# A two-layer transformer kernel: the second half's input normalisations on another engine, four low parts on VectorE, and a new table of places

## What is computed

```python
x = L0_attn_x                                  # (4, 256, 512) float32
xn = layernorm(x)
h = xn @ Win.T + bin                           # the small model: width 64, 4 layers
for l in range(4):
    h = h + sconv(silu(layernorm(h)), l) * sc_lin[l]      # a decaying complex scan
    h = h + silu(layernorm(h) @ W1[l].T + b1[l]) @ W2[l].T + b2[l]
small = layernorm(h) @ Wout.T + bout
hidden = silu(xn @ gate.T * gate_s) * (xn @ up.T * up_s)   # 1792 wide, codes -1, 0, 1
x = x + small + (hidden @ down.T) * down_s
xn = layernorm(x)
z = (silu(xn @ U1 @ V1g + b1g) * (xn @ U1 @ V1u + b1u)) @ U2 @ V2 + b2
x = x + xn @ (weight * block_mask).T + bias + z
```

## Time and profile before

| what | value |
|---|---|
| median of three runs | 305.38 us |
| profiled execution, its own time | 305.49 us |
| its span, first to last instruction | 303.6 us |
| TensorE busy | 291.7 us, 96% |
| VectorE busy | 175.8 us, 58% |
| GpSimd busy | 159.2 us, 52% |
| ScalarE busy | 118.4 us, 39% |
| mean granted TensorE clock | 0.977 of full |

### The profile page before, as it was taken

One profiled execution on the slowest core, in us unless ns is written; L12 is line 12 of the kernel. 1 busy time (PEld: TensorE's weight loads), 2 busy tenths in 40 slices (PEclk: granted clock), 3 DMA queues, 4 the chain that ended last, 5 costly groups with the idle time before them and its releaser, 6 DMA issues.

```text
span 303.6 us, 4378 instructions
## 1 busy us (share of the span) xinstructions
PE 291.7 (96%) x1573; PEld 194.3 (64%) x1573; DVE 175.8 (58%) x270; ACT 118.4 (39%) x197; POOL 159.2 (52%) x184
## 2 busy tenths in 40 slices
PE   6888989999999999999999999989999999999995
PEld 4785547665565657556565655646577888788784
DVE  3784796565725784684545745678887622333303
ACT  1552345453634132444635535223045730146500
POOL 4878259995391311155474284630467585047650
PEclk9795899999999999999999999999999999999999
DMA  7999618108000212010110011210020000200003
GB/s 256 328 286 208 101 35 124 33 1 121 2 0 2 69 36 71 0 35 13 37 35 26 2 35 38 69 35 2 0 69 1 3 1 32 73 35 0 0 2 138
DMA packets 11749, 17.86 MB, mean 59 GB/s; under 512 B 848, under 2 KB 6224, under 8 KB 11728
## 3 DMA queue, kind: packets, MB, share of 16 engines
q1 hardware_dynamic: 6624, 12.49, 12.7%
q0 software_dynamic: 4960, 4.98, 10.1%
q10 hardware_dynamic: 144, 0.12, 0.1%
HBM read 20.46 MB, written 2.10 MB: 74 GB/s over the span
## 4 chain that ended last, share of the span: by engine, by line
PE 85%; POOL 6%; DVE 4%; issue 2%; DMA 1%; ACT 1%; DVEq 0%; POOLq 0%
PE bank L593 15%; PE bank L594 15%; PE bank L690 15%; PE bank L561 8%; PE bank L563 8%; PE bank L562 8%; PE bank L652 5%; PE bank L624 3%; PE bank L630 2%; PE bank L555 2%; DMA early<-in_params 1%; PE bank L643 1%; PE bank L642 1%; PE bank L615 1%; POOL root L1079 1%
## 5 line engine op out<-in xcount | busy, mean ns | idle before, releaser
L1162 POOL TENSOR_TENSOR hidl<-hid,hidh 128x512 f16<-128x512 f32 x28 | 33.3, 1189 | 47.8 <-ACT hidh L756 47.6
L593 PE MATMUL bank<-xh,gatew 128*128 128x512 f16 (+1 forms) x136 | 45.5, 353 | 2.6 <-ACT XT L785 1.4
L594 PE MATMUL bank<-xl,gatew 128*128 128x512 f16 (+1 forms) x136 | 45.4, 353 | 0.0
L593 PE MATMUL bank<-xh,upw 128*128 128x512 f16 (+1 forms) x136 | 44.8, 348 | 0.0
L594 PE MATMUL bank<-xl,upw 128*128 128x512 f16 (+1 forms) x136 | 44.8, 348 | 0.0
L690 PE MATMUL bank<-downw,hidh 128*128 128x512 f16 x112 | 42.5, 380 | 0.0
L690 PE MATMUL bank<-downw,hidl 128*128 128x512 f16 x112 | 42.4, 379 | 0.0
L1168 POOL TENSOR_TENSOR actl<-hid,acth 128x512 fp32r<-128x512 f32 (+1 forms) x22 | 28.7, 1307 | 25.9 <-ACT acth L763 25.7
L1079 POOL TENSOR_TENSOR root<-var,powers 128x4 f32<-128x4 f32 (+1 forms) x25 | 23.6, 949 | 23.5 <-DVE var L942 19.9
L830 ACT ACTIVATE silu<-bank,early 128x512 f32<-128x512 f32 x28 | 19.2, 687 | 41.1 <-PE bank L594 41.1
L1011 DVE SCALAR_TENSOR_TENSOR hid<-bank,early,silu 128x512 f32<-128x512 f32 x28 | 21.0, 751 | 19.8 <-PE bank L594 19.3
(11 more groups left out here) (158 smaller groups left out, 607.1 us busy)
## 6 DMA issues: line engine op xcount, KB each, us to landing
X<-in_x SPq DMA_DIRECT2D x8, 256.0 KB, 5.6
out_x<-X SPq DMA_DIRECT2D x8, 256.0 KB, 2.0
downw<-in_down POOLq DMA_DIRECT2D x2, 896.0 KB, 8.3
stage<-in_v SPq DMA_DIRECT2D x6, 256.0 KB, 2.6
stage<-in_mask SPq DMA_DIRECT2D x4, 256.0 KB, 7.0
upw<-in_up POOLq DMA_DIRECT2D x1, 1024.0 KB, 11.9
gatew<-in_gate POOLq DMA_DIRECT2D x1, 1024.0 KB, 12.5
stage<-in_weight SPq DMA_DIRECT2D x4, 256.0 KB, 2.6
```

Source lines behind the costliest of these rows:

```text
L593: pe.matmul(bank_of(key)[:, c], w, xh[b][:, k, c], start=(k == 0), stop=False)
L594: mm = pe.matmul(bank_of(key)[:, c], w, xl[b][:, k, c], start=False, stop=(k == KT - 1))
L1162: pool.tensor_tensor(hidl[:, n % FT, :], hid[:, n % UNITS, :], hidh[:, n % FT, :], ALU.subtract).then_inc(hid_lo, 1)
```

## The change

- The four normalisations of block 1 in layer 0 move from VectorE to ScalarE, as an Identity activation with a scale (the root) and a bias (minus mean times root). VectorE makes minus the mean, GpSimd multiplies by the root (tile nmr).
- The low parts of units 0 to 3 move from GpSimd to VectorE, each behind the hid of the next unit, with a semaphore of their own (first_lo).
- The constants ahead of the first transpose are 15 instead of 11, and three more (FILL) stand ahead of the first pass.
- PROLOGUE is written anew; `rows` and `centre win` are in it now. All tables of places have new numbers.
- SyncE waits for the first casting load of gate codes before it issues the fifth staged load and what is behind it.

```diff
-    place(W2_AT, [[("rows",), ("centre", "win")], [("centre", "w2")]])
+    place(W2_AT, [[("centre", "w2")]])
...
-PROLOGUE = ((("seed", 0), ("stats", 0), ("stats", 1), ("norm", 0), ("seed", 1), ("norm", 1), ("stats", 2)),
-            (("xt", 0), ("codes", 0), ("load", 0), ("norm", 2), ("seed", 2), ("stats", 3), ("grow", 0)),
+PROLOGUE = ((("stats", 0), ("stats", 1), ("load", 0), ("norm", 0), ("seed", 0), ("stats", 2), ("norm", 1), ("seed", 1)),
+            (("xt", 0), ("codes", 0), ("norm", 2), ("seed", 2), ("stats", 3), ("grow", 0)),
             (("xt", 1), ("codes", 1), ("first", 0, 0), ("norm", 3), ("load", 1), ("grow", 1)),
-            (("xt", 2), ("first", 0, 1), ("xcopy", 0), ("first", 1, 0), ("grow", 2), ("grow", 3)),
-            (("xt", 3), ("first", 1, 1), ("xcopy", 1), ("first", 2, 0), ("first", 2, 1), ("xcopy", 2),
+            (("xt", 2), ("rows", 0), ("first", 0, 1), ("xcopy", 0), ("first", 1, 0), ("grow", 2), ("grow", 3)),
+            (("xt", 3), ("centre", 0), ("first", 1, 1), ("xcopy", 1), ("first", 2, 0), ("first", 2, 1), ("xcopy", 2),
              ("first", 3, 0), ("first", 3, 1), ("xcopy", 3)))
-WARM = 11
+WARM = 15
+FILL = 3
...
-LOAD_AT = (0.2, 0, 7.1, 16.2)
-GROW_AT = (0, 0, 0.1, 0.5, 0.5, 0.5)
-LN_AT = (0.1, 1.1, 1.2, 1.4, 1.7, 4.1, 4.4, 5.0, 6.4)
+LOAD_AT = (1.8, 1.9, 15.7, 12.9)
+GROW_AT = (0, 0, 0, 0, 0.6, 0.8)
+LN_AT = (0, 0, 0, 0, 0.4, 2.2, 4.7, 6.7, 8.4)
...
+            sp.wait_ge(codes_in[0], 16)
             for n in range(FIRST_LOADS, NSTAGE):
                 load(n)
...
+                    if (t, f) == (0, 0):
+                        for _ in range(FILL):
+                            constants()
...
+                if kind == "norm" and step[1:3] == (0, 1):
+                    t = step[3]
+                    act.wait_ge(nmr_ready, 1)
+                    wait_full(act, ("xt", 0, t))
+                    act.activation(XN[:, t, :], X[:, TPB + t, :], ACT.Identity, bias=nmr[:, 1, t:t + 1],
+                                   scale=root[NBLK][:, t:t + 1]).then_inc(xn_act, 1)
...
+                    if 1 <= n <= LOWS:
+
+                        dve.wait_ge(hid_hi, n)
+                        emit(dve.tensor_tensor(hidl[:, n - 1, :], hid[:, (n - 1) % UNITS, :], hidh[:, n - 1, :],
+                                               ALU.subtract), first_lo)
...
+                    if step[1:3] == (0, 1):
+                        pool.wait_ge(neg_ready, 1)
+                        pool.wait_ge(root_ready[NBLK], rooted[NBLK])
+                        pool.tensor_tensor(nmr[:, 1, :], nmr[:, 0, :], root[NBLK][:], ALU.mult).then_inc(nmr_ready, 1)
```

More of the change, by code:

```diff
@@ L56 @@
 UNITS = 3
+LOWS = 4
 FIRST = 2
@@ L163, in build_order @@
                       "codes": [("cast", "gate", t), ("cast", "up", t)], "seed": [("seed", t)],
-                      "first": [("first", t, *f)], "load": [("load", t)], "grow": [("grow", t)]}.get(kind, [(kind, 0, t)])
+                      "first": [("first", t, *f)], "rows": [("rows",)], "centre": [("centre", "win")], "load": [("load", t)], "grow": [("grow", t)]}.get(kind, [(kind, 0, t)])
     order.append(("decay",))
@@ new lines @@
+XCOPY_AT = (5.3, 7.4, 8.7, 10.0)
+W1_AT = (5.8, 7.4)
+W2_AT = (8.6,)
+WOUT_AT = (32.2,)
+XBIAS_AT = (22.6, 29.3)
+MASK_AT = (33.1, 37.8, 39.5, 41.3, 42.4)
+U1_CAST_AT = (45.3,)
+V1_AT = (48.1, 52.0, 56.9, 60.1, 65.6, 68.0)
+U2_AT = (73.0, 73.8, 75.3)
+CHAIN_AT = ((1.6, 5.3, 7.5, 7.5, 10.1, 11.4, 13.4, 14.2, 15.2, 17.4, 19.2, 21.4, 21.5, 26.1, 27.3, 28.9, 30.2, 32.6, 34.6, 35.5, 37.2, 37.9, 41.6, 44.4, 45.5, 45.8, 47.7, 50.0, 51.2, 53.7, 55.4, 58.2, 59.1, 61.0, 62.4, 63.7, 66.1, 69.6, 72.0, 73.1, 74.6, 75.5), (12.3, 14.4, 15.7, 16.3, 18.1, 19.6, 23.3, 24.5, 26.1, 27.3, 29.3, 31.3, 32.4, 35.0, 37.3, 38.6, 38.7, 41.5, 42.0, 44.7, 46.0, 46.0, 50.3, 52.9, 53.6, 54.6, 55.1, 58.3, 60.2, 61.3, 64.2, 66.7, 68.6, 69.5, 72.8, 74.4, 75.3, 76.1, 78.2, 78.7, 82.0, 82.5))
@@ L209, in place_psum @@
+WMASK_AT = (67.6, 69.3, 75.7, 75.9)
+W_AT = (82.3, 83.1, 85.4, 87.1)
+LN1_AT = ((76.0, 76.1, 76.1, 76.9, 76.9, 78.0, 78.4, 78.4, 78.4, 80.2, 81.0, 81.3, 82.1), (82.0, 86.3, 87.4, 90.0, 90.1, 91.6, 92.9, 93.4, 94.6, 95.5, 96.4, 97.7, 98.8))
+YBIAS_AT = ((99.7, 103.0, 104.8, 108.7), (111.4, 116.1, 128.2, 128.7))
+V2_AT = (88.4,)
 def place_psum(order):
@@ L595, in gate_up, with constants @@
                 return mm
+            def constants():
+                pe.matmul(banks[0][:], onesr[:], onesr[:, 0:1].to_broadcast([P, D]), start=True, stop=True)
             pe.wait_ge(ones_ready, 1)
             for _ in range(WARM):
-                pe.matmul(banks[0][:], onesr[:], onesr[:, 0:1].to_broadcast([P, D]), start=True, stop=True)
+                constants()
             pe.wait_ge(prm_in, 16)
@@ L604, in _ @@
                 if kind in ("xt", "yt"):
-                    layer = 0 if kind == "xt" else 1
-                    transpose_tile(step, xn_ready, (layer * NBLK + step[1]) * TPB + step[2] + 1)
+                    if step[0:2] == ("xt", 1):
+                        transpose_tile(step, xn_act, step[2] + 1)
+                    else:
+                        layer = 0 if kind == "xt" else 1
+                        transpose_tile(step, xn_ready, (layer + step[1]) * TPB + step[2] + 1)
                 elif kind == "win":
@@ L687, in _ @@
                             wait_codes(pe, "down", f)
-                            pe.wait_ge(hid_lo, unit(b, f) + 1)
+                            if unit(b, f) < LOWS:
+                                pe.wait_ge(first_lo, unit(b, f) + 1)
+                            else:
+                                pe.wait_ge(hid_lo, unit(b, f) + 1 - LOWS)
                         for part in (hidh, hidl):
@@ L893, in _ @@
                     n = b * TPB + t
+                    if (layer, b) == (0, 1):
+                        continue
                     dve.wait_ge(root_ready[NBLK], t + 1 if (layer, b) == (0, 0) else
@@ L1148, in _ @@
                         n = b * TPB + t
-                        pool.wait_ge(xn_ready, n + 1)
+                        if b == 0:
+                            pool.wait_ge(xn_ready, n + 1)
+                        else:
+                            pool.wait_ge(xn_act, t + 1)
                         pool.tensor_tensor(X[:, n, :], X[:, n, :], bc[:, BOUT, :],
@@ L1160, in _ @@
                     n = unit(step[1], step[2])
+                    if n < LOWS:
+                        continue
                     pool.wait_ge(hid_hi, n + 1)
```

40 lines of the change are left out of this document (16 added, 24 removed).

## The result

The changed kernel takes **301.38 us** (median of 4 runs, 301.28 to 301.81) beside 305.44 us (305.12 to 306.18) for the kernel before on the same chip: ratio 0.9866, interval 0.9846 to 0.9886. Forecast were 299.6 us, with a range of 297.0 to 303.4. The profiled execution took 301.28 us, its span is 299.5 instead of 303.6: 4.1 us less where the sum said 5.8.

The account below looks back on a forecast made before the run. TensorE, busy 96% of the span, was taken as the bound, its loose time lying ahead of 40 us. Terms -0.8 -1.2 -3.0 -3.2 +2.0 +0.4 = -5.8 us gave 299.6 us, range 297.0 to 303.4.

Parts of the forecast that it names:

- Part 1: Up to the first projection: rows and centring of win come earlier, so it starts at 19.9 instead of 20.67, -0.8 us.
- Part 2: Clock stays at 1.00 through the first projection: projection -1.2 us, half-clock matmuls and a transpose behind it -3.0 us.
- Rival 3: Gate codes land late, TensorE stalls and half clock may return: slower, 306.4 us, or 308 with late up codes; chance 0.05.
- Part 3: TensorE's two waits between the projections, for XN and for an XT copy, are removed: -3.2 us.
- New waits from ScalarE: Between the projections, XN now queued on ScalarE and the last XT copy make TensorE wait: 0.8, 0.15, 0.55, 0.5, sum +2.0.
- The cost of the low parts and of two engines at one memory: Ahead of the second projection, GpSimd stretches VectorE's four new low parts: +0.4 us on TensorE's path.
- Loads: Gate and up codes of units 6 to 13, W1, bc and masks still land in time: no cost.
- Behind the second projection: From about 48 us on all engines move up alike, with no new wait and the tail unchanged.
- 1 (no new waits): ScalarE and VectorE slip through earlier, so the new waits don't appear: -8.2 us, 297.2 us; chance 0.15.
- 2 (the clock falls anyway): Clock falls around the first projection for another cause than the gap: 303.3 us; chance 0.15.
- 4: The head start is lost later, on VectorE or GpSimd: 305 us; chance 0.05.
- gap (d): TensorE's standstill up to 40.0 us in the kernel before, waiting for an XT copy on ScalarE; counted as 1.5 us.

Follow-up runs that it names:

- a_cold: The changed kernel with 11 warming matmuls instead of 15 and none of the three fillers: 301.65 us, ratio 0.9866 to the kernel before.
- a_gap: The changed kernel with rows, the centring of win and two statistics back in the old order: 305.24 us, ratio 0.9997 to the kernel before.
- r_rows: The kernel before with only rows and the centring of win moved to the change's places: 306.66 us, ratio 1.0026.
- a_normdve: The changed kernel with block 1's four normalisations (XN) back on VectorE at the same steps: 306.79 us, ratio 1.0052 to the kernel before.
- a_nosp: The changed kernel without SyncE's wait for the first gate codes: 301.50 us, ratio 0.9875 to the kernel before.
- a_tables: The changed kernel with GpSimd's second table product and the second part of W1 moved behind the scan: 300.06 us, ratio 0.9814 to the kernel before.
- a_lows0: The changed kernel with the first four low parts back on GpSimd: 300.22 us, ratio 0.9835 to the kernel before.
- c_tablow0: The changed kernel with the edits of a_tables and a_lows0 together: 300.87 us, ratio 0.9842 to the kernel before.
- a_best: a_tables with other places for the tables, silu of unit 1, a GpSimd root and the fourth XN: 299.76 us, ratio 0.9821 to the kernel before.
- a_best2: a_best with one table product moved from ahead of a root to an idle stretch of GpSimd: 298.93 us, ratio 0.9769 to the kernel before.
- c_bestlow0: a_best with all low parts back on GpSimd: 302.92 us, ratio 0.9912 to the kernel before.

## Why the prediction was right in kind and short in size

Faster was right, and the likeliest case named the places; it missed by 1.8 us, inside its own 301.5 by 0.1. By its steps, with places and times of the profiled pair:

- **Part 1** (-0.8): -0.86, right. The profiled pair shows -1.27, but 0.41 of it is the earlier x, which is also most of why the projection starts at 19.40 and not at 19.9. The forecast took the fillers at the half-clock pitch and they ran at 0.22 (8.95 on, clock 1.00); that changed nothing, since a_cold, which leaves them out, has the same 15.44 us from the first statistics to the projection.
- **Part 2** (-1.2, -3.0): right in the profiled pair: 3.68 for the projection, clock 1.00 to the end. The step that took the gap for what lowers the clock holds only in part: with a gap of 1.87 us a_gap's clock stayed up in three timed runs of ten and in both profiled ones. The Trainium skill (TensorE: Matmul & The Clock Gate, "HAM oscillation — how this bites in real kernels") looks for the cause in long idle gaps; r_rows and a_normdve, with gaps of 6.73 and 5.87 us, bear it out, and the short gap is a risk rather than a cause. In runs of the kernel before, the mean clock was 0.976 to 0.994, never higher; in all 29 runs of the change, a_nosp, a_tables, a_lows0, c_tablow0, a_best and a_best2, which have no such gap, it was 0.998 to 1.00. Two of a_cold's four runs, without such a gap but without the extra constants too, had 0.994. Rival 3's stall of "over some 1.5 us" rests on no row of that length: here 1.87 and 2.35 us left the clock up in their traces.
- **Part 3** (-3.2): both old waits went. The product nmr was ready at 24.76, where the replay had 24.75 (luck by 0.4: in c_tablow0, where x lands as late as in the trace of before, it was ready at 25.19), and the XN on ScalarE took 0.81 (0.78 was taken).
- **New waits from ScalarE** (+2.0): 0.9, 0.1, 0.6 and 0.65, 2.25 in all. Right in size; the last, for the XT copy, goes with a_tables, so it too came from VectorE being late.
- **The cost of the low parts and of two engines at one memory** (+0.4): this is the term that was mis-sized. It was bounded for the four low parts alone, and taken near its low end because GpSimd was mostly "in small operations or idle". The traces show 1.7 us on TensorE's path (0.5 for lno, 1.2 for ymini). Up to the end of the scan VectorE's rows are 3.0 us longer than the shortest of their kind, 0.75 of it in low parts and the rest in what stands around them, the scan above all (1.3), beside a table product and a part of W1 that the new places had put there. The row that the forecast took its bounds from had a warning in it: 0.75 at its fastest, but 1.52 in the median, so the stretch was the usual case. a_tables takes GpSimd's work away, and a cast with it, and gives 1.3 us back; a_lows0 gives 1.2. The Trainium skill (SBUF — State Buffer, "SBUF: two separate sides") has one of these engines wait out the other's instruction; the forecast gave -4.5 by it, without a working, and the time fell by 4.1. The trace agrees with the rule: what is waited for is the rest of an instruction under way, which the ends 0.28 and 0.55 us behind GpSimd's show, and of the four low parts only the one beside the W1 part had such a rest to wait out (1.15). The first and the last took 0.69, and beside the first it was a small product of GpSimd that took 0.51 instead of 0.20; the second, 0.98, lay beside the issue of a load.
- **Loads**: the gate codes took 9.1 us instead of 9.5, the up codes 14.4; both in time. **Behind the second projection**: no wait that was not there, as said.
- **Rivals.** 1 (no new waits) fell, as the waits are all there. 2 (the clock falls anyway) was not seen in any of the 4 runs. 3 and 4 fell. The mechanism of a slower case was in none of them: r_rows and a_normdve are slower than before by a long wait that lowers the clock behind it.

The sum of the measured steps with the earlier x in it, -1.3 -1.2 -3.0 -3.2 +4.0 = -4.7, is 0.3 more than the 4.4 seen at the second projection; where these 0.3 are stays open. So do two things of the clock: why it fell at 23.1 in the kernel before and not at gap (d), and where it falls in the slower runs of a_gap.

## What to carry to other kernels

A head start of one stage was worth nothing here until the next stage's input came earlier too (r_rows): find who gives it, and move that first. Count places in a trace from the first instruction that waits for an input, and not from zero, or an input that lands earlier looks like a gain. When work goes from one engine to another, list what the third engine has in hand beside each instruction it will delay or stretch, and put long elementwise work of GpSimd where VectorE isn't on the path, or beside those of its operations that read a PSUM bank, which never stretched here. Undo parts of a change together as well as singly: here two parts that cost 1.3 and 1.2 us were worth only 0.5 when both were undone.

## What the runs showed of the hardware

- Two scans of 128x256 f32 on VectorE took 1.39 us with GpSimd idle (a_tables) and 2.71 beside its table product and W1 part (1.05 and 1.54 us); the product ahead of them 0.69 and 0.99, a low part 0.69 to 1.15, in a_best 1.67 beside a W1 part, and in c_bestlow0 a 128x256 operation 2.93 instead of 0.42.
- These stretched rows end 0.55 us (the 128x256 operation and the casts 0.28) behind the GpSimd instruction beside them. VectorE operations that read a PSUM bank (hid, xl, lno) had the same time beside GpSimd as alone.
- Waits of TensorE of 6.73 and 5.87 us were followed by the 1.2 GHz level; one of 1.87 us was not in two profiled executions, and its kernel's runs fell into three groups by mean clock, 1.4 us apart.
- An activation with scale and bias from memory took 0.81 us at 128x512 f32, a copy 0.60.
